# Graph layer with routed experts: sorted rows copied by SP run by run, shorter row rounds, carried tiles in one sequence

## Chip, cores and metric

One core of one Trainium2 chip. The metric is the device time of one execution in microseconds. Before the change it is 2572.58 us (median of 3 runs, 2572.57 to 2572.97).

## What is computed

One layer over 6250 nodes of 256 features and 206250 edges sorted by destination:

```python
xn = layernorm(x)
x = x + graph_attention(xn, src, dst) + linear_attention_mix(xn)
z = layernorm(x) * gamma + beta
logits = z @ Wr + br                       # 8 experts
top_vals, top_idx = top_k(logits, 2); w = softmax(top_vals)
y = sum over both picks of w * (gelu(z @ W1[e] + b1[e]) @ W2[e] + b2[e])
x = x + y
```

The graph attention has 4 heads of 64: each edge fetches its source row, gets a softmax weight among the edges of its destination, and is added to it. The last three lines are the routed experts (256 to 512 to 256).

## The kernel before

**Edge loop.** The edges are cut into 403 blocks of 512. For block n, POOL issues four indirect gathers (L1113, 128 rows of 264 floats each) into one of four buffers; it first waits until PE is through with block n - 4 (`block_ps`). DVE forms logits (L1542 to L1544), ACT takes the exponential (L1179), DVE adds the former block to the accumulator (L1558, twice), weighs the selection matrix (L1550) and prepares the mask three blocks ahead (L1530 to L1534), and PE multiplies, 32 small products (L1303). Each engine's program is in order, written out by hand. After the steps of a block (`body`) come whatever other steps have that block's number: up to block 151 those of the mixing stage, from block 152 (FREE_FROM) the row rounds and the carried tiles.

**Row rounds.** Destinations are finished in order, so finished nodes leave the loop in rounds of 7 tiles of 128 rows (SIZES; the seventh has 4, the eighth 3). A round has steps u = 0 to 35, one a block from its start in STARTS: u 0 SP issues 16 loads of sums and two of rows (`sums`, `sync`, L261 to L268); u 4 ACT scales (28 activations, L314); u 5 DVE adds and inverts (L388, L389); u 6 ACT scales again (28, L321); u 7 DVE adds (L393), SP stores; u 8, 9 statistics (L397); u 10, 11 the deviation; u 12 to 28 in pairs of tiles: ACT normalizes into `sent_rows` (L331), PE turns the tile, PE multiplies by Wr, DVE reads the logits (L410); u 29, 30 DVE picks two experts; u 31 PE counts; u 32, 33 DVE works out each row's slot; u 35 the list of expert tiles that are full (`tile_list`). Rounds 0 to 5 start at blocks 152, 191, 230, 270, 309 and 349; round 6 (4 tiles) starts at 382 and has its steps packed into 18 blocks. Round 7 runs in the tail.

**Sending.** Each tile's rows go to `expert_in`, in which each expert has its own range, in two indirect scatters by POOL (`scatter`, L287), one for each row's first and second expert, 128 rows of 258 floats (the row, its node number, its gate). The table SENDS puts them behind POOL's gathers: one tile a block in the first 7 blocks of the next round.

**Carried tiles.** 28 of the 56 expert tiles of 256 rows are computed inside the loop (`carried_part`), seven after each list, at STARTS[q + 2] + 10, one every 5 blocks: SP loads rows and weights (L600 to L605), PE turns and multiplies, DVE copies b1 and gates and scales (L667 to L670), ACT applies gelu, DVE adds b2 and multiplies by the gate (L678, L679), SP stores (L610). The other 28 are computed in the tail, in which PE works and POOL gathers the carried results and adds the others to the output (L2152, L2162).

## Time and profile before

| | |
|---|---|
| median of the runs | 2572.58 us |
| profiled execution | 2576.69 us, of which the span of the core's instructions is 2575.0 us |
| busy | PE 1533.0 us (60%), DVE 1492.4 (58%), ACT 680.0 (26%), POOL 1852.0 (72%) |
| granted TensorE clock, mean | 0.672 of full speed |
| DMA | 441.85 MB, mean 172 GB/s; queue of POOL 35.9% of 16 engines' span, queue of SP and ACT 23.1% |

Busy times leave out register, semaphore and DMA-issuing instructions of SP and ACT. An indirect DMA of POOL counts as busy while POOL makes its descriptors. "Idle before" is the time for which the engine stood before an instruction, with what ended it; "issue" means that the profile shows nothing it waited for.

### The profile page before, as it was taken

What the parts mean: (1) busy time and instruction counts of PE and PEld (TensorE: products, weight loads), DVE (VectorE), ACT (ScalarE), POOL (GpSimd) and SP (SyncE); (2) the same over time, 40 slices, a digit from 0 to 9 for tenths busy, and PEclk for the clock granted to TensorE, in tenths of its full rate; (3) what the DMA queues carried; (4) which work ended last, traced back from release to release, by engine and by line L of the source; (5) the groups of instructions that cost most, each with busy time, mean ns of one, the idle gap of its engine ahead of it and who ended that gap; (6) DMA issues with size and microseconds to landing.
All of it is one profiled execution on the core that took longest, in us unless ns stands there. A gap on an engine that the chain in (4) does not pass through costs nothing. (4 is left out here: it accounts for less than half of the span.)

```text
span 2575.0 us, 53300 instructions
## 1 busy us (share of the span) xinstructions
PE 1533.0 (60%) x17219; PEld 1189.0 (46%) x17219; DVE 1492.4 (58%) x5566; ACT 680.0 (26%) x2013; POOL 1852.0 (72%) x1872
## 2 busy tenths in 40 slices
PE   5676665556666445335425664765675475648993
PEld 4444434444444333224324553554564364537882
DVE  5666656667777565444645665575567666534333
ACT  3332221122222131032123224323322433322220
POOL 1677777777777777777777777777777777746673
PEclk9688865666555555555556775777676676778997
DMA  9477775645555644544456675557557656557986
GB/s 303 130 205 200 199 202 145 177 113 144 161 155 149 166 118 109 150 118 108 109 146 174 181 206 169 160 162 202 171 162 206 198 164 192 163 167 201 249 225 205
DMA packets 301706, 441.85 MB, mean 172 GB/s; under 512 B 73686, under 2 KB 227752, under 8 KB 301292
## 3 DMA queue, kind: packets, MB, share of 16 engines
q0 software_dynamic: 94320, 246.50, 35.9%
q1 hardware_dynamic: 197980, 183.38, 23.1%
q10 hardware_dynamic: 9120, 8.48, 1.0%
q8 instruction: 141, 2.31, 0.4%
q14 instruction: 145, 1.19, 0.1%
HBM read 361.39 MB, written 72.13 MB: 168 GB/s over the span
## 5 line engine op out<-in xcount | busy, mean ns | idle before, releaser
L1113 POOL DMA_INDIRECT region<-node_table,src_idx x1612 | 1576.0, 978 | 503.2 <-issue 475.1
L1303 PE MATMUL ps_p<-region 128*32 128x65 f32 x12896 | 389.3, 288 | 440.7 <-DVE region L1550 438.4
L1303 PEld LDWEIGHTS ps_p<-region 128*32 128x32 f32 x12896 | 301.0, 150 | 540.7 <-DVE region L1550 531.8
L1285 PE MATMUL ps_s<-ident,region 128*128 128x128 f32 x403 | 167.5, 416 | 427.3 <-DVE region L1544 417.2
L1179 ACT ACTIVATE ps_p<-region 128x16 f32<-128x16 f32 x403 | 75.4, 187 | 1249.6 <-DVE region L1544 1242.7
L1558 DVE SCALAR_TENSOR_TENSOR acc<-ps_p,region,acc 128x65 f32 x806 | 193.2, 280 | 285.2 <-issue 279.2
L1550 DVE TENSOR_TENSOR region<-region,ps_p 128x512 f32<-128x512 f32 x403 | 273.5, 679 | 49.9 <-ACT ps_p L1179 48.3
L1285 PEld LDWEIGHTS ps_s<-ident,region 128*128 128x128 f32 x403 | 87.7, 217 | 458.7 <-DVE region L1544 447.2
L1542 DVE TENSOR_TENSOR region<-region,ps_s 128x16 f32<-128x16 f32 x403 | 68.0, 169 | 284.5 <-DMA region<-node_table,src_idx 248.6
L1289 PEld LDWEIGHTS ps_s<-region 128*128 128x128 f32 x806 | 199.6, 278 | 60.9 <-issue 34.9
L1175 ACT ACTIVATE region<-ps_s 128x128 f32<-128x128 f32 x403 | 111.1, 276 | 303.7 <-PE ps_s L1285 303.3
L1289 PE MATMUL ps_s<-region 128*128 128x32 f32 x806 | 189.7, 325 | 0.2 <-ACT region L1175 0.2
L1531 DVE SCALAR_TENSOR_TENSOR region<-drep,region 128x8 f32<-128x8 f32 x403 | 91.7, 228 | 64.5 <-DVE region L1530 64.5
L2227 PE MATMUL ps_eu<-region 128*128 128x256 f32 x448 | 112.7, 409 | 24.1 <-DVE region L2271 17.3
L287 POOL DMA_INDIRECT expert_in<-acc x98 | 100.6, 1027 | 30.1 <-issue 30.1
L2162 POOL DMA_INDIRECT out_dram<-acc,rows_of x56 | 90.7, 1620 | 42.8 <-issue 42.5
L1530 DVE TENSOR_SCALAR region<-drep,region 128x8 f32 x403 | 103.2, 256 | 20.5 <-issue 15.6
L1534 DVE TENSOR_TENSOR region<-region 128x128 f32<-128x128 f32 x403 | 114.3, 284 | 0.0
L2227 PEld LDWEIGHTS ps_eu<-region 128*128 128x128 f32 x448 | 91.7, 207 | 41.2 <-DVE region L2271 18.8
L1319 PE MATMUL ps_x<-region 128*128 128x384 f32 x196 | 106.3, 680 | 0.0
L2239 PE MATMUL ps_ey<-region 128*128 128x256 f32 x448 | 101.3, 379 | 0.0
L2152 POOL DMA_INDIRECT acc<-y_rows,acc x70 | 70.0, 1000 | 41.7 <-issue 20.7
(347 smaller groups left out, 2477.5 us busy)
## 6 DMA issues: line engine op xcount, KB each, us to landing
region<-in_W_dram SPq DMA_DIRECT2D x84, 512.0 KB, 5.5
region<-node_table,src_idx POOLq DMA_INDIRECT x1612
acc<-in_W_dram SPq DMA_DIRECT2D x28, 512.0 KB
region<-expert_in SPq DMA_DIRECT2D x47, 258.0 KB, 5.6
acc<-base_rows SPq DMA_DIRECT2D x13, 896.0 KB, 7.3
qkv_rows<-region SPq DMA_DIRECT2D x49, 194.0 KB
y_rows<-acc SPq DMA_DIRECT2D x28, 256.0 KB
node_table<-region SPq DMA_DIRECT2D x49, 132.0 KB, 4.7
```

The source lines that it names most:

```text
L1113: pool.indirect_dma_start(out=rows[:, s, j, :], out_offset=None, in_=table[:, :], in_offset=bass.IndirectOffsetOnAxis(ap=src_idx[:, n * SU ...
L1175: act.activation(maskT[:, s % 2, :], ps_s[s % 2][:, 0:P], ACT.Copy).then_inc(maskT_ready, 1)
L1285: pe.transpose(ps_s[s % 2][:, 0:P], mask[:, s % SL].rearrange("p j w -> p (j w)"), ident[:, :]).then_inc(maskT_ps, 1)
L1289: pe.matmul(ps_s[s % 2][:, 2 * P:2 * P + SUB * 8], maskT[:, s % 2, :], dsel[:, s % SL].rearrange("p j c -> p (j c)"), start=True, stop=Tru ...
L1303: m = pe.matmul(ps_p[s % 2][h * WIN:(h + 1) * WIN, 0:HC], wts[:, s % 2, j, h, :], rows[:, s, j, h * HC:(h + 1) * HC], start=j == 0, stop=j ...
L1319: m = pe.matmul(ps_x[2 + a % 2][:, 0:3 * HID], xT_tiles[:, a % XT, c, :], w_q[:, c, :], start=c == 0, stop=c == KC - 1)
L1530: own.do(dve.tensor_scalar(t8[:, 0, :], drep[:, bass.ds(c, 1), :].squeeze(1), here[:, 0, at(n)], None, ALU.mult))
L1534: own.do(dve.tensor_tensor(mask[:, s % SL], bcast(rel[:, bass.ds(n * SUB, SUB)], 2, WIN), bcast(win, 1, SUB), ALU.is_equal))
L1550: dve.tensor_tensor(wts[:, s % 2], bcast(mask[:, s], 2, G_HEADS), bcast(ex_ps(s), 3, WIN), ALU.mult).then_inc(w_ready, 1)
L1558: m = dve.scalar_tensor_tensor(out=a, in0=ps_p[s % 2][:, 0:HC], scalar=here[:, k, at(n)], in1=a, op0=ALU.mult, op1=ALU.add)
L2227: m = pe.matmul(ps_u[2 * (n % 2) + f // 2][:, (f % 2) * MT:(f % 2 + 1) * MT], w1s[n % WS][:, c, f * P:(f + 1) * P], xeT[:, n % 2, c, :], s ...
L2239: m = pe.matmul(ps_y[n % 2][:, b * DIM:(b + 1) * DIM], hidT[:, n % 2, c, b * P:(b + 1) * P], w2s[n % WS][:, c, :], start=c == 0, stop=c == ...
```

## The change

Rounds 0 to 4 (35 tiles) no longer scatter through POOL. Behind u 33 of such a round each tile is sorted by expert: DVE builds a 128 x 256 selection matrix from the two picks (steps 33 + 2j), PE multiplies it with the tile in two halves (34 + 2j, 35 + 2j), ACT copies each half out of PSUM (35 + 2j, 36 + 2j), SP writes 256 sorted rows to `run_rows` in DRAM (37 + 2j). Then SP copies, expert by expert, 128 rows from where that expert's run begins to where its next free slot begins, DRAM to DRAM, with both addresses from a register: 8 copies a tile, two a block (`send_runs`). The rows beyond the run's end are overwritten by the next tile's, so a half of four experts waits until the same half of the tile before has landed. Rounds 5, 6 and 7 still scatter (now one row buffer for both picks).

A row now holds 260 floats: the values, node number, first expert, second weight, and first minus second weight. The carried part and the tail work out the gate from these (`weigh_rows`, two more DVE operations a tile, with an own column of `b1T` for the expert's number). The steps u 0 to 33 of rounds 0 to 4 are packed into 22 blocks (table AT), several in one block, and the rounds start at 152, 189, 226, 263 and 300; round 5 stays at 349 and round 6 at 382. The 28 carried tiles stand in one sequence, every 5 blocks from block 257 to 392. At the front, SP loads b1 in four pieces and fills the spare rows of `run_rows`, 0.9 MB.

```diff
-MROW = DIM + 2
+MROW = DIM + 4
+TURNED = 5
+TURN_U = 33
+SLOT = 5 * P
...
+        j = turn(r, u, 4)
+        if j is not None:
+            m = r.m + j
+            turned_out.wait(sp, 2 * (m + 1))
+            if m >= GT:
+                for half in run_out:
+                    half.wait(sp, HALF_RUNS * (m - GT + 1))
+            sp.dma_start(run_rows[j * SLOT:j * SLOT + 2 * P, :].rearrange("(c p) d -> p c d", p=P),
+                         sorted_rows[:, m % 2]).then_inc(run_in[m % 2].sem, 16)
     part.sync = sync
+
+    def send_runs(sp, r, q):
+        j, part_of = divmod(q, 4)
+        m = r.m + j
+        if part_of == 0:
+            run_in[m % 2].wait(sp, 16 * (m // 2 + 1))
+        landed = run_out[part_of // 2]
+        if m and part_of % 2 == 0:
+            landed.wait(sp, HALF_RUNS * m)
+        for e in range(2 * part_of, 2 * part_of + 2):
+            v = sp.value_load(run_at[0:1, j * E + e:j * E + e + 1], min_val=0, max_val=N_PAD * 512 + 511)
+            to = expert_in[e * CAP:(e + 1) * CAP, :][bass.ds(v >> 9, P), :]
+            sp.dma_start(to.rearrange("(a b) c -> a (b c)", a=16),
+                         run_rows[j * SLOT:(j + 1) * SLOT, :][bass.ds(v & 511, P), :].rearrange("(a b) c -> a (b c)", a=16)).then_inc(landed.sem, 16)
+    part.send_runs = send_runs
...
+    def turn(r, u, d):
+
+        k = u - TURN_U - d
+        return k // 2 if r.turned and 0 <= k < 2 * r.gt and k % 2 == 0 else None
+
+    def turn_half(r, u, d):
+
+        k = u - TURN_U - d
+        return divmod(k, 2) if r.turned and 0 <= k < 2 * r.gt else None
...
-            act.activation(sent_rows[:, j, :, 0:DIM], bcast(x_all[:, j, :], 1, 2), ACT.Identity,
+            act.activation(sent_rows[:, j, 0:DIM], x_all[:, j, :], ACT.Identity,
...
+        j = turn_half(r, u, 2)
+        if j is not None:
+            j, c = j
+            m = r.m + j
+            turned.wait(act, 2 * m + c + 1)
+            if m >= 2 and c == 0:
+                run_in[m % 2].wait(act, 16 * (m // 2))
+            act.activation(sorted_rows[:, m % 2, c, :], ps[3][:, 0:MROW], ACT.Copy).then_inc(turned_out.sem, 1)
...
+        j = turn_half(r, u, 1)
+        if j is not None:
+            j, c = j
+            m = r.m + j
+            if c == 0:
+                chosen.wait(pe, m + 1)
+            if m or c:
+                turned_out.wait(pe, 2 * m + c)
+            pe.matmul(ps[3][:, 0:MROW], sel[:, m % 2, c * P:(c + 1) * P], sent_rows[:, j, :], start=True, stop=True).then_inc(turned.sem, 1)
...
+            if r.turned:
+                if r.m:
+                    runs_landed(dve, r.m)
+                runs = run_te.rearrange("p (t e) -> p t e", e=E)[:, 0:n]
+                spot3 = spot_te.rearrange("p (t e) -> p t e", e=E)[:, 0:n]
+                own.do(dve.tensor_tensor_scan(run_te, mask_te[:, :], ps[3][:, DIM:DIM + n * E], 0.0, ALU.mult, ALU.add))
+                own.do(dve.tensor_tensor(runs, runs, total, ALU.subtract))
+                own.do(dve.tensor_tensor(spot3[0:1], pos[0:1], bcast(cap[0:1, :], 1, n), ALU.subtract))
+                own.do(dve.scalar_tensor_tensor(out=run_at[0:1, :], in0=spot_te[0:1, :], scalar=512.0, in1=run_te[0:1, :], op0=ALU.mult, op1=ALU.add))
+                own.do(dve.tensor_tensor(spot3, runs, ps[3][:, 0:n * E].rearrange("p (t e) -> p t e", e=E), ALU.add))
...
+                if r.turned:
+                    own.do(dve.tensor_tensor(work, oh, spot_te.rearrange("p (t e) -> p t e", e=E)[:, 0:n], ALU.mult))
+                    own.do(dve.tensor_reduce(spots[:, c, 0:n], work, AX.X, ALU.add))
...
+        j = turn(r, u, 0)
+        if j is not None:
+            m = r.m + j
+            if m >= 2:
+                turned.wait(dve, 2 * (m - 1))
+            own.do(dve.tensor_scalar(sel[:, m % 2, :], spot[:, :], spots[:, 0, j:j + 1], None, ALU.is_equal))
+            dve.scalar_tensor_tensor(out=sel[:, m % 2, :], in0=spot[:, :], scalar=spots[:, 1, j:j + 1], in1=sel[:, m % 2, :],
+                                     op0=ALU.is_equal, op1=ALU.add).then_inc(chosen.sem, 1)
...
+def weigh_rows(dve, own, gates, choice, expert):
+
+    own.wait()
+    own.do(dve.scalar_tensor_tensor(out=gates, in0=choice[:, :, 0], scalar=expert, in1=choice[:, :, 2], op0=ALU.is_equal, op1=ALU.mult))
+    own.step(dve.tensor_tensor(gates, gates, choice[:, :, 1], ALU.add))
...
-    CARRY_AT, CARRY_STEP = 10, 5
-    STARTS = [FREE_FROM + d for d in (0, 39, 78, 118, 157, 197)]
-    STEPS = {s + u: [(k, u)] for k, s in reversed(list(enumerate(STARTS))) for u in range(ROWS_U)}
+    CARRY_AT, CARRY_STEP = BLOCKS - 146, 5
+    STARTS = [FREE_FROM + d for d in (0, 37, 74, 111, 148, 197)]
+    AT = (0, None, None, None, 3, 3, 5, 5, 6, 6, 7, 8, 9, 9, 10, 10, 11, 11, 12, 12, 13, 13, 14, 14, 15, 15, 16, 16, 17, 17, 18, 19,
+          20, 21)
+    TURN_AT = AT[TURN_U]
+    STEPS, RUN_STEPS = {}, {}
+    for k, s in enumerate(STARTS):
+        if k < TURNED:
+            for u in range(TURN_U + 4 + 2 * GT):
+                d = AT[u] if u < len(AT) else TURN_AT + u - TURN_U
+                if d is not None:
+                    STEPS.setdefault(s + d, []).append((k, u))
+            for q in range(4 * GT):
+                RUN_STEPS[s + TURN_AT + 5 + q] = (k, q)
+        else:
+            for u in range(ROWS_U):
+                STEPS.setdefault(s + u, []).append((k, u))
...
-    for k in range(EARLY - 2):
-        for j in range(SIZES[k]):
-            SENDS.setdefault(STARTS[k + 1] + j, []).append((k, j))
...
-            for q in range(4):
-                d = n - v - STARTS[q + 2] - CARRY_AT
-                if 0 <= d < CARRY_STEP * CARRY and d % CARRY_STEP == 0:
-                    return q * CARRY + d // CARRY_STEP
-            return None
...
+                if n in RUN_STEPS:
+                    k, q = RUN_STEPS[n]
+                    part.send_runs(sp, early_round(k), q)
                 m = carry_at(n, -2)
                 if m is not None:
-                    carried.sync(sp, m, (m // CARRY + 2) * (2 * GT * 16))
+                    carried.sync(sp, m, (m // CARRY + 2) * GT)
```

POOL's order behind the front of the program, before: gathers for the edges (L1113) and scatters to expert_in (L287), here the last two tiles of one round and the first of the next.

```order
L287 DMA expert_in<-acc 54272x258 x2
L1113 DMA region<-node_table,src_idx 128x264 x4
L287 DMA expert_in<-acc 54272x258 x2
L1113 DMA region<-node_table,src_idx 128x264 x132
L287 DMA expert_in<-acc 54272x258 x2
```

And with the change, where L1244 is the gather and L332 the scatter:

```order
L1233 MEMSET acc 128x1792 x2
L1244 DMA region<-node_table,src_idx 128x264 x1552
L332 DMA expert_in<-acc 54272x260 x4
L1244 DMA region<-node_table,src_idx 128x264 x4
L332 DMA expert_in<-acc 54272x260 x4
```

The first 388 blocks' gathers now follow one another with nothing between.

ACT's order at the start of round 0, before: L1179 and L1175 are the exponential and the mask's copy of a block, L314 and L321 the 28 scalings of u 4 and u 6.

```order
L314 ACTIVATE acc<-acc,w_self 128x65 x28
L1179 ACTIVATE ps_p<-region 128x16
L1175 ACTIVATE region<-ps_s 128x128
L1179 ACTIVATE ps_p<-region 128x16
L1175 ACTIVATE region<-ps_s 128x128
L321 ACTIVATE acc<-acc 128x64 x28
L1179 ACTIVATE ps_p<-region 128x16
L1175 ACTIVATE region<-ps_s 128x128
```

And DVE's order there with the change: the end of the body of block 3 (L1665, L1666), u 5 (L464, L465), then the next body (L1674 on).

```order
L1665 TENSOR_TENSOR region<-bm,region 128x32
L1666 TENSOR_TENSOR region<-region 128x128
L464 TENSOR_TENSOR acc<-acc 128x1820
L465 RECIPROCAL acc<-acc 128x28
L1674 TENSOR_TENSOR region<-region,ps_s 128x16
L1675 SCALAR_TENSOR_TENSOR region<-region 128x16
```

Before, u 5 stood one body behind the block in which ACT does u 4; now it stands at the end of that same block, and u 7 likewise in the block of u 6.

## Rows read from the trace of the kernel before

**Rows 1.** Page, groups: line, engine, operation, count | busy us, mean ns | idle before, releaser

```profile
L1113 POOL DMA_INDIRECT region<-node_table,src_idx x1612 | 1576.0, 978 | 503.2 <-issue 475.1
```

**Rows 2.** Timeline of POOL: start us, us, instruction [idle before <- releaser]

```profile
726.05 0.95 POOL L1113 DMA_INDIRECT region<-node_table,src_idx  x1 [1.93 <-PE ps_p L1303]
...
1069.33 0.95 POOL L1113 DMA_INDIRECT region<-node_table,src_idx  x1 [0.30 <-issue]
1070.58 1.01 POOL L287 DMA_INDIRECT expert_in<-acc  x1 [0.31 <-issue]
```

**Rows 3.** Waits (us in total, times, longest): whole run; 873:1452; 1452:2271

```profile
POOL region L1113 <- PE ps_p L1303: 20.2, 52, 1.9
...
DVE region L1542 <- DMA region<-node_table,src_idx: 141.2, 68, 7.0
...
DVE region L1542 <- DMA region<-node_table,src_idx: 50.1, 27, 5.3
```

**Rows 4.** POOL's groups in 873:1452 and 1452:2271; windows (PE, PEld, DVE, ACT, POOL busy, PEclk, DMA, GB/s)

```profile
L1113 POOL DMA_INDIRECT region<-node_table,src_idx x424 | 414.0, 977 | 129.2 <-issue 123.1 <-PE ps_p L1303 6.1
L287 POOL DMA_INDIRECT expert_in<-acc x28 | 27.9, 996 | 8.5 <-issue 8.5
...
L1113 POOL DMA_INDIRECT region<-node_table,src_idx x575 | 561.3, 976 | 175.2 <-issue 171.9 <-PE ps_p L1303 3.4
L287 POOL DMA_INDIRECT expert_in<-acc x56 | 57.9, 1034 | 17.1 <-issue 17.1
...
873.00:1452.00 579.00, 262.57 (x3903) 200.56 (x3904) 302.76 (x1222) 138.80 (x470) 441.30 (x452) 0.53 0.49 137
1452.00:2271.00 819.00, 504.38 (x6128) 407.19 (x6126) 509.78 (x1968) 262.36 (x731) 619.25 (x631) 0.70 0.61 177
2271.00:2575.00 304.00, 224.64 (x1094) 192.75 (x1094) 112.22 (x312) 64.29 (x153) 176.19 (x142) 0.87 0.77 217
```

**Rows 5.** Timeline: logits and products of one block; logits of another and the next

```profile
895.81 0.17 DVE L1542 TENSOR_TENSOR region<-region,ps_s 128x16 f32<-128x16 f32 x1 [3.25 <-DMA region<-node_table,src_idx]
...
898.19 1.09 PE L1303 MATMUL ps_p<-region 128*32 128x65 f32 x32 [1.26 <-DVE region L1550]
...
1179.15 0.17 DVE L1542 TENSOR_TENSOR region<-region,ps_s 128x16 f32<-128x16 f32 x1 [1.41 <-DMA region<-node_table,src_idx]
...
1184.17 0.17 DVE L1542 TENSOR_TENSOR region<-region,ps_s 128x16 f32<-128x16 f32 x1 [1.72 <-DMA region<-node_table,src_idx]
```

**Rows 6.** DVE's groups in 1452:2271: steps of the rounds and the carried tiles

```profile
L670 DVE TENSOR_SCALAR acc<-ps_x,affine 128x256 f32<-128x256 f32 x49 | 24.3, 537 | 0.2 <-issue 0.2
...
L678 DVE TENSOR_TENSOR acc<-ps_x,acc 128x512 f32<-128x512 f32 x26 | 18.0, 692 | 6.3 <-PE ps_x L654 2.5 <-DVE region L1534 2.1 <-DVE acc L444 0.9
L397 DVE BATCH_NORM_STATS2 acc<-acc 128x6 f32<-128x256 f32 x25 | 8.6, 412 | 0.6
...
L667 DVE COPY acc<-b1T 128x4 f32 x24 | 4.9, 203 | 23.0 <-DVE region L1534 11.3 <-issue 4.1 <-DVE acc L410 2.9
...
L437 DVE TENSOR_TENSOR acc<-acc 128x56 f32<-128x56 f32 (+1 forms) x10 | 2.1, 214 | 0.9
```

**Rows 7.** Timeline at u 4 and u 5 of round 0

```profile
897.14 6.81 ACT L314 ACTIVATE acc<-acc,w_self 128x65 f32<-128x65 f32 x28
...
904.04 0.69 DVE L1550 TENSOR_TENSOR region<-region,ps_p 128x512 f32<-128x512 f32 x1 [2.83 <-ACT ps_p L1179]
...
905.99 2.06 DVE L388 TENSOR_TENSOR acc<-acc 128x1820 f32<-128x1820 f32 x1
906.32 2.55 POOL L1113 DMA_INDIRECT region<-node_table,src_idx  x1 [0.30 <-issue]
```

**Rows 8.** Timeline at the start of round 6, of 4 tiles

```profile
2150.43 0.17 DVE L1542 TENSOR_TENSOR region<-region,ps_s 128x16 f32<-128x16 f32 x1
2152.17 10.33 SPq L261 DMA_DIRECT2D acc<-acc  x16
...
2170.38 3.95 ACT L314 ACTIVATE acc<-acc,w_self 128x65 f32<-128x65 f32 x16 [6.84 <-DMA acc<-base_rows]
```

More of the change, by code:

```diff
@@ L204 @@
 EARLY_TILES = sum(SIZES[:EARLY])
-MAIN_SENT = sum(SIZES[:EARLY - 1])
+MAIN_TURNED = sum(SIZES[:TURNED])
+MAIN_SENT = sum(SIZES[TURNED:EARLY - 1])
+HALF_RUNS = 8 * EXPERTS
 EARLY_PAIRS = pairs_in(SIZES[:EARLY])
@@ L275, in sync @@
         elif u == 8:
-            if r.k:
+            if r.m:
+                turned.wait(sp, 2 * r.m)
+            if r.s:
                 sp.wait_ge(sent, 32 * r.s)
@@ L281, in sync, with runs_landed @@
             sp.wait_ge(n_ready, r.t + n)
-    part.sync = sync
+        j = turn(r, u, 4)
[7 more added lines that the diff above has]
+                         sorted_rows[:, m % 2]).then_inc(run_in[m % 2].sem, 16)
+    part.sync = sync
+    def send_runs(sp, r, q):
[12 more added lines that the diff above has]
+    part.send_runs = send_runs
+    def runs_landed(eng, tiles):
+        for half in run_out:
+            half.wait(eng, HALF_RUNS * tiles)
     def scatter(pool, r, j):
@@ L353, in tensor @@
             pe.wait_ge(n_ready, r.t + (j + 1))
+            if j == 0 and r.m:
+                turned_out.wait(pe, 2 * r.m)
             if j >= 2:
@@ L415, in vector @@
             pick(dve, own, n, lg, 0, first)
+            own.do(dve.tensor_copy(sent_rows[:, 0:n, DIM + 1], gate))
         elif u == 30:
@@ L552, in list_at @@
     if q < 4:
[L553 removed]
+        return g["carry_e"][:, q, :], g["carry_s"][:, q, :]
     first = sum(LISTS[4:q])
@@ L590, in carried_part, with sync @@
     carried.first_landed = first_landed
-    def sync(sp, m, sent_count):
+    def sync(sp, m, tiles):
         q, s = m // CARRY, m % 2
         listed.wait(sp, q + 1)
-        sp.wait_ge(sent, sent_count)
-        v = sp.value_load(carry_s[0:1, q % 2, m % CARRY:m % CARRY + 1], min_val=0, max_val=EXPERTS * CAP + (EXPERTS - 1) * MT)
+        for half in run_out:
+            half.wait(sp, HALF_RUNS * tiles)
+        v = sp.value_load(carry_s[0:1, q, m % CARRY:m % CARRY + 1], min_val=0, max_val=EXPERTS * CAP + (EXPERTS - 1) * MT)
         if m >= 2:
@@ L672, in vector @@
             i.then_inc(xeT_ready.sem, 1)
+            weigh_rows(dve, own, gates[:, m % 4, :], choice[:, m % 4], b1s[:, m % 4, FC:])
         elif v == 8:
@@ L915, in main_stage @@
         row_loads = sem("row_loads")
+        g["row_sems"].update(chosen=Since(stats, X_GROUPS), turned=Since(sqrts, X_GROUPS), turned_out=Since(weights, 2),
+                             run_in=[Since(table_out[i], 16 * XG * ((X_GROUPS + 1 - i) // 2)) for i in range(2)],
+                             run_out=[Since(src_in, 16), Since(dst_in, 32)])
         part = rows_part(g, g["row_sems"], ps_x)
@@ L1392, in _ @@
                     carry_sems["listed"].wait(pe, LISTED)
+                    part.turned_out.wait(pe, 2 * MAIN_TURNED)
                     send_notes(g, pe, ps_x[3], noted_ps)
@@ L1844, in round_of @@
                     part.sums(sp, early_round(k, 1))
-                    for u in range(ROWS_U):
+                    for u in range(TURN_U + 4 + 2 * GT):
                         part.sync(sp, early_round(k, 1), u)
+                        j, due = divmod(u - TURN_U - 5, 2)
+                        if k < TURNED and 0 <= j < GT and due == 0:
+                            for q in range(4 * j, 4 * j + 4):
+                                part.send_runs(sp, early_round(k, 1), q)
                 for k in range(EARLY - 1):
@@ L1870, in rest @@
             def rest():
-                for k in range(EARLY - 1):
+                for k in range(TURNED, EARLY - 1):
                     for j in range(SIZES[k]):
@@ L1890, in round_of @@
                 def round_of(k):
-                    for u in range(ROWS_U):
+                    for u in range(TURN_U + 4 + 2 * GT):
                         part.scalar(act, early_round(k, 1), u)
@@ L1917, in round_of @@
                 def round_of(k):
-                    for u in range(ROWS_U):
+                    for u in range(TURN_U + 4 + 2 * GT):
                         part.tensor(pe, early_round(k, 1), u)
@@ L1973, in round_of @@
                 def round_of(k):
-                    for u in range(ROWS_U):
+                    for u in range(TURN_U + 4 + 2 * GT):
                         part.vector(dve, own, early_round(k, 1), u)
@@ L2273, in rows_back @@
                 m.then_inc(xeT_ready, 1)
+                weigh_rows(dve, own, gates[:, n % MS, :], choice[:, n % MS], b1s[:, n % MS, FC:])
             def result(n):
```

121 lines of the change are left out of this document (74 added, 47 removed).

## The prediction

> **What bounds the kernel now.** I read the page's groups of instructions, then the waits of the whole run and of two stretches, then single blocks in the timeline. The edge loop runs 403 blocks, and POOL issues four gathers for each. The idle time ahead of its gathers is "issue" for 475 of 503 us [rows 1]: it waits for nobody, it needs 0.95 us for a gather and 0.30 us to reach the next [rows 2]. PE holds it up for 20.2 us in all [rows 3]. So in the loop a thing taken off POOL's queue is worth its issue time, as long as DVE keeps pace. That condition decides here, so I split the free part of the loop where the carried tiles become dense.
>
> Stretch A (873 to 1452 us, blocks 152 to 256, 105 blocks): 579 us, of which DVE waits 141.2 us for gathered rows [rows 3]. DVE's chain (its own work, and what it waits for from ACT and PE) needs 579 - 141 = 438 us. Stretch B (1452 to 2271 us, blocks 257 to 402): 819 us, DVE waits for gathers only 50.1 us [rows 3], so the chain needs 769. POOL's own need without any scatter, and without its waits for PE, is 579 - 36.4 - 6.1 = 537 us in A and 819 - 75.0 - 3.4 = 741 in B: the window less busy and idle time of L287 and less PE's part of L1113's [rows 4]. **In A POOL has 99 us over DVE; in B, without scatters, DVE's chain is the longer one already, 769 against 741.**
>
> **What goes.** 70 scatters leave POOL: all 28 of A's and 42 of B's 56; the order shows the last 14 alone between gathers. One costs 36.4/28 = 1.30 us in A and 75.0/56 = 1.34 in B [rows 4]: 36.4 and 56.2 us, 92.6 together. In B at most the 50 us of gather waits can come away, even if nothing were added.
>
> **What is added on DVE's chain.** A block without other steps takes it 1184.17 - 1.72 - 1179.15 = 3.3 us [rows 5]; of the 5.03 us that POOL gives a block, 1.7 are free in A.
> - Selection: two operations over 128x256 a tile. I take 0.8 us for both with their waits, nearest to two of L397 at 0.41; bounds 0.5 and 1.4 (two at 0.69) [rows 6]. Further small steps in u 29, 32 and 33, about ten at 0.21 [rows 6] plus gaps: 2.7. A turned round: 7 x 0.8 + 2.7 = 8.3 us.
> - weigh_rows: two small operations and a wait, 0.5 us a carried tile, 14 for 28.
> - Three more carried tiles fall into B (28 against 25). One is two of L670 at 0.54, two of L678 at 0.69 and two small ones at 0.2, 2.9 us of work [rows 6]; with its waits (23.0/24 = 1.0 ahead of L667 alone) I take 5: 15 us.
> - **Compression puts u4 with u5, and u6 with u7, in one block.** ACT's 28 scalings take 6.8 us and begin 897.14 - 895.81 = 1.3 us behind DVE's logits [rows 5, 7]. Before, DVE did a block meanwhile and lost only the late exponential, 2.8 us ahead of L1550 [rows 7]. Now it stands until 8.1 us instead of 3.3: 4.8 us each time, net 2 more.
> - u4 comes 3 blocks after the loads, not 4. At the one place where it came after 2, SP issued from 2152.17 and ACT could start at 2170.38: 18.2 us [rows 8]. SP starts 1.8 us after the block's logits (2150.43), so data are there 20 us behind them; three blocks are 15.1, and with ACT's 1.3 the new wait is 3.6 us in A, about 3 in B.
>
> B's chain: 769 + 2 rounds x 8.3 + 1.6 (last turns of round 2) + 14 + 15 + 2 x (2 x 2 + 3) = 830, less 13 for the end of round 2 (u 29 to 35, some 50 small steps at 0.21 and a gap), which moves ahead of block 257, plus 10 for the gather waits that stay where DVE is not late: 827. **B: +8 us.**
>
> A: POOL's 537, plus stalls. POOL may be four blocks ahead: from the end of a block's gathers to the first that needs its buffer are 0.3 + 3 x 5.03 = 15.4 us, and PE's products end 898.19 + 1.09 - 895.81 = 3.5 us after a block's logits begin [rows 5], so DVE may be 11.9 us late. It is 1.8 us late when all is well. Blocks 3 to 6 of a compressed round take 4.9 + 6.8 + 2.4 = 14.1, 3.3, 1.3 + 6.8 + 2.4 = 10.5, and 3.3 + 7 x 0.41 + 6 x 0.21 = 7.5 us [rows 5 to 7] (L393 and L321 taken like L388 and L314): 35.4 against 20.1, so 15.3 later, 17.1 in all, 5.2 over the limit. Such a stall exists now, 1.93 us [rows 2]. Three rounds: 16 us. With 2 us for a late chain at the boundary: 555. **A: -24 us.**
>
> Outside the loop: the tail's 28 tiles are paced by PE (busy 225 of 304 us [rows 4]); weigh_rows hides there, unless DVE becomes late, 0.5 us a tile, 14 at most. I take 0. The loads at the front hide behind the mixing stage: 0 to 5.
>
> **Work off the chain.** SP issues 280 copies. A plain issue is 10.33/16 = 0.65 us [rows 8]; even at twice that for the register loads, two a block are 2.6 of 5 us, so SP holds. A copy moves 128 x 260 x 4 = 133 KB; 35 tiles x 8 are 37 MB read and 37 written, with run_rows' own 266 KB 1.33 MB a tile read. That is about 45 GB/s more on A's 137 and 28 on B's 177, at DMA shares of 0.49 and 0.61 [rows 4]: no bound; a gather may land later, which four buffers cover in A. PE gets two 128x260 products a tile, an estimated 0.5 us each, with PE busy 263 of 579 us in A and 504 of 819 in B [rows 4].
>
> A gather that meets DVE's 2.06 us sum over 128x1820 takes 2.55 instead of 0.95 us [rows 7]. The Trainium skill (SBUF — State Buffer, "SBUF: two separate sides") says why: DVE and GpSimd share one port pair, held for a whole instruction. The trace agrees. By it all 70 new selections would hit POOL, up to 0.8 us a tile, 28 us, 17 of them in A. The rows bound it lower: L1113 averages 978 ns against 950 over all that DVE does [rows 1, 2], 0.03 us a gather, so under 2 us here, left out.
>
> Moving the scatters to SP saves issue time alone, and issue time is what POOL is short of: 1.3 us each [rows 4]. The Trainium skill (DMA: Bandwidth & Descriptors, "Issuing engines are not separate DMA queues") speaks against the change: another issuing engine saves only the sequencer's time, "usually small relative to the DMA itself". The rows do not agree for POOL; by the rule alone the sum would be about 0.
>
> **Sum.** -24 + 8 = -16 us, on the profiled execution's 2576.69 us: 2560.7. The median of the runs is 4.1 us below that execution, so I predict **2556.5 us**. A measurement of this kernel can tell 0.2%, 5 us.
>
> **Rivals.**
> - *Inputs late (slower).* Each round's 18 loads share SP and the rings with the former round's copies, and my row (18.2 us) is of a 4-tile round; 7-tile loads with copies ahead could be 5 to 9 us longer. DVE stands behind ACT in that block, so 5 rounds x 5 to 9 us = 25 to 45: 2582 to 2602. It decides from 16/5 = 3 us a round. For: SP's waits sit in one queue. Against: in round 0, of 7 tiles, ACT found the data after four blocks without a wait [rows 7]. Chance 0.25.
> - *Added work hides (faster).* ACT's and PE's part in B's 769 is waiting, and what is inserted falls into it: B's chain grows by 15, not 58, so B gives -30, all -54 with A: 2518 to 2535. Chance 0.17.
> - *POOL alone counts.* All 92.6 come away, 2480. Against it stand B's 50 us. Chance 0.03.
> - *No change.* Gains and costs cancel within 5 us, by contention, the port or the tail. Chance 0.13.
> - My forecast, 2540 to 2567: 0.42.
>
> The range that leaves out 2 in 10 is 2525 to 2590. Faster by over 0.2%: 0.42 + 0.17 + 0.03 = 0.62; same 0.13; slower 0.25.
>
> **What would show it.** In the profile after, the gathers' group keeps 0.98 us and its "issue" time, but waits for PE 40 to 100 us, against 20 now, in bursts 5 to 10 blocks after each round's start; 28 scatters instead of 98; DVE's wait for gathers falls from 141 to about 60 in A and from 50 to about 10 in B; block 257 comes near 1428 us, 24 earlier, the loop's end near 2255, only 16 earlier. If POOL waits for PE under 20 us in all, the chain was priced too high and the time is near 2500; if ACT's first scaling waits over 8 us for its loads in each round, the slower rival holds.

## The result and the profile after

The changed kernel takes **2589.49 us** (median of 4 runs), the kernel before 2572.57 on the same chip: a ratio of 1.0058, 95% interval 1.0043 to 1.0073. It is slower by 17 us where I forecast 16 faster. The profiled execution has a span of 2587.5 us.

The gathers' group on the page after, beside [rows 1], with the queue that takes SP's copies (packets, MB, share of 16 engines) and the group of DVE's first operation on gathered rows:

```profile
q1 hardware_dynamic: 217420, 231.05, 28.9%
...
L1244 POOL DMA_INDIRECT region<-node_table,src_idx x1612 | 1576.0, 978 | 615.2 <-issue 471.1
...
L1674 DVE TENSOR_TENSOR region<-region,ps_s 128x16 f32<-128x16 f32 x403 | 68.0, 169 | 164.5 <-DMA region<-node_table,src_idx 120.0
```

A gather costs what it did, 978 ns, and POOL's "issue" (idle for which the profile shows no cause) is 471.1 us against 475.1. What grew is the rest of the idle time: 615.2 - 471.1 = 144 us, against 28 before. POOL is rid of 70 scatters and now waits for others.

The waits of stretch A (872 to 1438 us, blocks 152 to 256) and of B (1438 to 2288, blocks 257 to 402), beside [rows 3] (who <- whom: us, times, longest):

```profile
DVE region L1674 <- DMA region<-node_table,src_idx: 59.0, 38, 4.6
DVE acc L464 <- ACT acc L371: 34.4, 3, 12.6
POOL region L1244 <- PE ps_p L1434: 28.8, 10, 3.5
ACT acc L371 <- DMA acc<-base_rows: 19.9, 3, 7.6
```

```profile
POOL region L1244 <- PE ps_p L1434: 99.2, 38, 9.5
DVE acc L464 <- ACT acc L371: 36.4, 3, 18.5
PEld ps_x L742 <- DMA region<-expert_in: 22.3, 2, 13.6
ACT acc L371 <- DMA acc<-base_rows: 14.3, 2, 8.4
DVE region L1674 <- DMA region<-node_table,src_idx: 8.6, 3, 4.6
```

DVE's waits for gathers fell to 59.0 and 8.6, as forecast (60 and 10). But L371, ACT's scalings of u4, now waits for the row loads in rounds 0 to 3 (7.6, 6.9, 5.4 and 8.4 us; the fifth wait, 5.9, is round 6's, which had one before too). L742, PE's transposes of a carried tile's rows, waits 13.6 us in one place. POOL's groups in the two stretches, beside [rows 4]:

```profile
L1244 POOL DMA_INDIRECT region<-node_table,src_idx x424 | 411.5, 971 | 155.2 <-issue 126.4 <-PE ps_p L1434 28.8
```

```profile
L1244 POOL DMA_INDIRECT region<-node_table,src_idx x576 | 562.9, 977 | 263.5 <-issue 164.3 <-PE ps_p L1434 99.2
L332 POOL DMA_INDIRECT expert_in<-acc x14 | 13.8, 982 | 4.3 <-issue 4.3
```

Block by block (from the timeline, the start of DVE's first operation on a block's logits) the time went like this. The rows begin at the starts of rounds 0, 1, 2, 4 and 5 and at block 257, where B begins; round 3 starts at 263. The last three columns are experiments, of which more below; their control is the column "again", c1_after.

| blocks | before | change | again | c3_lead2 | c2_all | e5_scatters |
|---|---|---|---|---|---|---|
| 152 to 189 | 189.3 | 198.4 | 197.4 | 191.5 | 190.0 | 197.6 |
| 189 to 226 | 208.3 | 197.6 | 197.9 | 194.1 | 189.8 | 208.2 |
| 226 to 257 | 182.1 | 169.6 | 170.2 | 164.5 | 166.0 | 177.2 |
| 257 to 300 | 235.9 | 248.1 | 246.7 | 261.7 | 246.1 | 246.9 |
| 300 to 349 | 274.9 | 300.9 | 304.4 | 291.4 | 283.4 | 295.9 |
| 349 to 402 | 308.0 | 300.5 | 302.1 | 300.1 | 304.5 | 306.5 |
| sum | 1398.4 | 1415.2 | 1418.8 | 1403.3 | 1379.8 | 1432.4 |

A is 14 us faster (forecast 24), B is 31 us slower (forecast 8). 26 of B's 31 lie in blocks 300 to 349; of the rest, 12 were lost in 257 to 300 and 7.5 won back behind 349.

A round's start in the timeline: round 0, block 152, whose logits are at 872.32; block 155's are at 888.2 (start, us, engine, line, idle before):

```profile
874.13 11.54 SPq L276 DMA_DIRECT2D acc<-acc  x16
885.71 0.60 SPq L282 DMA_DIRECT2D acc<-node_table  x1
886.36 0.66 SPq L283 DMA_DIRECT2D acc<-base_rows  x1
...
897.25 6.82 ACT L371 ACTIVATE acc<-acc,w_self 128x65 f32<-128x65 f32 x28 [7.62 <-DMA acc<-base_rows]
...
904.10 2.06 DVE L464 TENSOR_TENSOR acc<-acc 128x1820 f32<-128x1820 f32 x1 [12.57 <-ACT acc L371]
904.73 2.25 POOL L1244 DMA_INDIRECT region<-node_table,src_idx  x1 [0.30 <-issue]
```

From SP's first issue to ACT's start are 23.1 us, with no copies of an earlier round about; I had taken 18.2 from a 4-tile round. The second run of the same kernel (c1_after) has 21.7 there. ACT starts u4 9.1, 8.4, 6.8, 10.0 and 15.0 us behind the block's logits in rounds 0 to 4, and 9.7 in the uncompressed round of block 349; with data in time it is 1.3. In rounds 0 to 3 the row loads release it, in the last two PE does. The block with u4 and u5 takes 18.6, 17.9, 16.3, 19.5 and 26.6 us, forecast 14.1.

Round 4, block 300, whose logits are at 1686.03, is the dearest. A carried tile's rows (L709) are asked for in the same block as the row loads:

```profile
1687.79 12.08 SPq L276 DMA_DIRECT2D acc<-acc  x16
1699.91 0.60 SPq L282 DMA_DIRECT2D acc<-node_table  x1
1700.55 0.66 SPq L283 DMA_DIRECT2D acc<-base_rows  x1
1702.33 2.25 SPq L321 DMA_DIRECT2D expert_in<-run_rows  x2
1705.50 0.41 SPq L709 DMA_DIRECT2D region<-expert_in  x1
...
1709.28 5.78 SPq L321 DMA_DIRECT2D expert_in<-run_rows  x4
1712.22 0.71 PEld L742 LDWEIGHTS ps_x<-ident,region 128*128 128x128 f32 x4 [13.62 <-DMA region<-expert_in]
...
1713.91 0.28 ACT L1306 ACTIVATE region<-ps_s 128x128 f32<-128x128 f32 x1 [14.02 <-PE ps_s L1416]
1714.08 6.80 ACT L371 ACTIVATE acc<-acc,w_self 128x65 f32<-128x65 f32 x28
```

The request leaves SP's queue 19.5 us after the block's logits, behind 18 loads and two copies. PE stands until it lands; ACT stands behind PE's transposes, DVE behind ACT. A sequence of step 5 meets them at 300 and, one block off, at 350 (8.7 us at 2014). Before, the carried tiles were tied to the rounds' starts, and one request alone fell behind row loads of its own block: at 382, the same 4-tile round from which I read the loads' time. There PE waited 6.2 us:

```profile
2164.59 0.39 SPq L600 DMA_DIRECT2D region<-expert_in  x1
...
2171.15 0.71 PEld L633 LDWEIGHTS ps_x<-ident,region 128*128 128x128 f32 x4 [6.19 <-DMA region<-expert_in]
```

### The profile page after: what moved, and what is told of

It reads as the page before. It is cut to its first block and busy times, and to the rows that moved or that the text cites. A ratio compares the mean times of both kernels' runs of the same rounds, so it can differ in the third digit from the quotient of the medians.

```text
span 2587.5 us, 56527 instructions
## 1 busy us (share of the span) xinstructions
PE 1584.4 (61%) x17359; PEld 1232.6 (48%) x17359; DVE 1546.6 (60%) x5813; ACT 690.4 (27%) x2083; POOL 1780.0 (69%) x1803
## 5 line engine op out<-in xcount | busy, mean ns | idle before, releaser
L1244 POOL DMA_INDIRECT region<-node_table,src_idx x1612 | 1576.0, 978 | 615.2 <-issue 471.1
L1416 PEld LDWEIGHTS ps_s<-ident,region 128*128 128x128 f32 x403 | 95.4, 237 | 428.4 <-DVE region L1676 419.7
L1420 PEld LDWEIGHTS ps_s<-region 128*128 128x128 f32 x806 | 205.9, 280 | 59.1 <-issue 27.9
L1420 PE MATMUL ps_s<-region 128*128 128x32 f32 x806 | 182.2, 316 | 0.0
L1674 DVE TENSOR_TENSOR region<-region,ps_s 128x16 f32<-128x16 f32 x403 | 68.0, 169 | 164.5 <-DMA region<-node_table,src_idx 120.0
L1666 DVE TENSOR_TENSOR region<-region 128x128 f32<-128x128 f32 x403 | 114.5, 284 | 0.0
L2380 PEld LDWEIGHTS ps_ey<-region 128*128 128x128 f32 x448 | 83.9, 192 | 10.8
```

Source lines behind the costliest of these rows:

```text
L1244: pool.indirect_dma_start(out=rows[:, s, j, :], out_offset=None, in_=table[:, :], in_offset=bass.IndirectOffsetOnAxis(ap=src_idx[:, n * SU ...
L1416: pe.transpose(ps_s[s % 2][:, 0:P], mask[:, s % SL].rearrange("p j w -> p (j w)"), ident[:, :]).then_inc(maskT_ps, 1)
L1420: pe.matmul(ps_s[s % 2][:, 2 * P:2 * P + SUB * 8], maskT[:, s % 2, :], dsel[:, s % SL].rearrange("p j c -> p (j c)"), start=True, stop=Tru ...
L1666: own.do(dve.tensor_tensor(mask[:, s % SL], bcast(rel[:, bass.ds(n * SUB, SUB)], 2, WIN), bcast(win, 1, SUB), ALU.is_equal))
L2380: m = pe.matmul(ps_y[n % 2][:, b * DIM:(b + 1) * DIM], hidT[:, n % 2, c, b * P:(b + 1) * P], w2s[n % WS][:, c, :], start=c == 0, stop=c == ...
```

## The experiments

The experiments ran on five chips, of two kinds. On one the kernel before takes 2577 us, near the 2573 of the prediction; c1, c2, c3 and e5 ran there. On four others, the slower chips, it takes 2969 to 3010, 15 to 17% more in every run. Ratios are to the kernel before on the same chip.

| run | edit | before, us | this, us | ratio (95%) |
|---|---|---|---|---|
| c1_after | the change again | 2577.4 | 2596.5 | 1.0075 (1.0050 to 1.0099) |
| c3_lead2 | u4 on two blocks later | 2577.4 | 2583.5 | 1.0022 (1.0008 to 1.0037) |
| c2_all | all three edits | 2577.4 | **2555.2** | 0.9916 (0.9894 to 0.9939) |
| e5_scatters | scatters kept | 2577.4 | 2608.2 | 1.0122 (1.0100 to 1.0145) |
| k1_after | the change again | 3000.9 | 2979.1 | 0.9929 (0.9912 to 0.9945) |
| e1_lead2 | u4 on two blocks later | 3009.5 | 2979.2 | 0.9896 (0.9875 to 0.9918) |
| e2_carry3 | carried tiles 3 blocks earlier | 3009.5 | 2986.7 | 0.9921 (0.9904 to 0.9937) |
| c4_carry3 | same | 3003.6 | 2978.7 | 0.9919 (0.9898 to 0.9941) |
| e3_split | double steps apart | 3009.5 | 2953.1 | 0.9809 (0.9793 to 0.9825) |
| c5_split | same | 3003.6 | 2948.5 | 0.9816 (0.9799 to 0.9832) |
| k2_split | same | 3000.9 | 2950.8 | 0.9830 (0.9814 to 0.9847) |
| m1_split | same | 2969.1 | 2912.8 | 0.9803 (0.9774 to 0.9832) |
| e4_all | all three | 3009.5 | 2947.4 | 0.9790 (0.9774 to 0.9807) |
| e6, k3, m2 | all three, scatters kept | 3003.6, 3000.9, 2969.1 | 3002.4, 3002.3, 2973.2 | 0.9996, 1.0003, 1.0012 |
| e7_early, k4_early | loads and carried rows earlier | 3003.6, 3000.9 | 2939.1, 2940.3 | 0.9785, 0.9796 |

**Loads further ahead.** The steps from u4 on come two blocks later, the loads stay:

```diff
-    AT = (0, None, None, None, 3, 3, 5, 5, 6, 6, 7, 8, 9, 9, ...
+    AT = (0, None, None, None, 5, 5, 7, 7, 8, 8, 9, 10, 11, 11, ...
```

> The changed kernel, whose steps from u 4 on come two blocks later in the five compressed rounds (u 4 and 5 at block 5 after the row loads, not 3); u 0, the loads, stay. Theory 'inputs late': the 18 loads land 24 us behind the block's logits, so ACT waits 7.6, 6.9, 5.4 and 8.4 us for them in rounds 0 to 3. Then these waits fall under 1 us, PE's products are held up less and POOL's waits for PE in blocks 152 to 256 fall from 28.8 to 5 to 15 us; round 4 keeps the 13.6 us of PE's wait for the carried tile's rows. Time 2562 to 2577. Rival 'DVE's chain is too long anyway' (selection, weighing, carried tiles): the wait was cover for nothing and only moves, ACT's waits go but the time stays within 5 us of 2589. Rival 'loads are slowed by the copies': they still land after 5 blocks, ACT still waits over 3 us.

> As e1_lead2 (u 4 and later steps two blocks later), on this chip: late inputs give 12 to 27 us less than the changed kernel beside it, and ACT's waits of 7.6, 6.9, 5.4 and 8.4 us for the loads in rounds 0 to 3 fall under 1; if these waits only covered DVE's own length, within 5 us of it.

It took 13 us off its control (2596.5 to 2583.5). Stretch A and its waits in c1_after, then in c3_lead2:

```profile
L1244 POOL DMA_INDIRECT region<-node_table,src_idx x423 | 412.2, 975 | 153.5 <-issue 126.0 <-PE ps_p L1434 27.5
```

```profile
L1243 POOL DMA_INDIRECT region<-node_table,src_idx x423 | 413.0, 976 | 138.3 <-issue 126.8 <-PE ps_p L1433 11.5
```

ACT starts 1.3 us behind the logits in rounds 0 to 2, the double block is 10.8 us in all three (16.5, 17.6 and 18.5 in the control), POOL waits 16.0 us less for PE, and A is 15.5 us shorter (565.6 to 550.1). That settles A: late loads were its cause. B gained nothing, 853.2 us in both. The steps now met carried rows in round 3, where PE waited 6.5 us at 1484 for the first time, and 11.3 in round 4; blocks 257 to 300 got 15 us longer, 300 to 349 13 shorter. On a slower chip the edit gave 0.9896 (e1_lead2), against 0.9929 for the unedited change on another of them (k1_after).

**Carried tiles three blocks earlier**, `BLOCKS - 149` for `BLOCKS - 146`:

> The changed kernel with its sequence of 28 carried tiles three blocks earlier (first at block 254, not 257). Theory 'one sequence collides with the row loads': at block 300 the carried tile's rows are asked for in the same block as the row loads and stand behind their 18 issues in SP's queue, so PE waits 13.6 us for them, and again about 8 us at block 350. Then PE's wait for these rows falls from 22.3 us to under 4 and the time by 8 to 17 us: 2572 to 2581. Rival 'ACT would have waited for the row loads in that block anyway': PE's wait goes, ACT's first scaling of round 4 waits 8 us instead, the gain is 2 to 7 us, 2582 to 2588. Rival 'rings full': the rows land as late as before, no gain.

> As e2_carry3 (carried tiles from block 254, nothing else), where the kernel before takes 2573 to 2577. The changed kernel gives 1.0058 to 1.0075 of it. If PE's wait for the rows of the carried tile (22.3 us, of which 13.6 at block 302) is what row loads at 300 and 349 cost, 8 to 17 us less: a ratio of 0.999 to 1.003. c3_lead2 showed 4 other blocks of that kind appear when the rounds' steps move (PE waited 25.7 us there and stretch B gained nothing), so the other outcome, under 4 us less, is likelier than I thought: it would say that the rows are late wherever SP's queue has 18 loads ahead of them.

It ran only on the slower chips. In c4_carry3 PE's wait for the rows fell to 5.4 us (19.3 in k1_after), and the time did not move against that control (0.9919 and 0.9921, 0.9929). There the wait goes and nothing is gained that these comparisons, each on its own chip, could show. The third outcome (the rows land as late as before) is out, since the wait went. ACT's wait for the row loads rose from 8.8 to 14.1, which speaks for the second. On the faster chip it was not tried alone.

**Double steps apart**: u4, 5, 6, 7 in blocks 3, 4, 5, 6, all later ones a block later.

```diff
-    AT = (0, None, None, None, 3, 3, 5, 5, 6, 6, 7, 8, ...
+    AT = (0, None, None, None, 3, 4, 5, 6, 7, 7, 8, 9, ...
```

> The changed kernel with u 4 and 5, and u 6 and 7, in separate blocks (3, 4, 5, 6 after the loads), all later steps one block later. By the term of my sum (4.8 us each time DVE stands behind ACT's 28 scalings, net 2 more than apart) DVE gets the body of a block meanwhile: 5 rounds x 2 x 2 = 20 us off DVE's chain, of which POOL shows what is over its slack: 8 to 20 us, 2570 to 2582. Theory 'inputs late' alone: ACT's wait for the loads stays 5 to 10 us a round since u 4 stays where it is, and gives 2578 to 2586. Rival 'no effect, the block behind needs ACT's exponential in any case': within 5 us of 2589.

> As e3_split (u 4, 5, 6, 7 in blocks of their own, the loads three blocks ahead as in the changed kernel). c2_all took 41 us off the changed kernel and c3_lead2 13, so splitting and the earlier carried tiles share 28 us. If DVE's standing behind ACT's 28 scalings was the larger part, this gives 15 to 28 us less than the changed kernel (ratio to the kernel before 0.996 to 1.001), with ACT's waits for the loads unchanged at 5 to 9 us but DVE's wait for ACT before u 5 (34.4 us in A, 36.4 in B) under 10 in each. If lateness is all, under 8 us.

> u 4, 5, 6, 7 in blocks of their own, nothing else. On the two slower chips it gave most of what all three edits gave (0.981 and 0.9816 against 0.979). Where the kernel before takes 2573 to 2577: if the double steps are the larger part, 15 to 28 us less than the changed kernel, 0.996 to 1.001; if late loads are, under 8 us less, over 1.003.

> u 4, 5, 6, 7 in blocks of their own, nothing else; k1_after and k2_split showed 28 us for it where the kernel before takes 3001 (2979 to 2951). Where it takes 2573 to 2577: with the double steps as the larger part 15 to 28 us less than the changed kernel, 0.996 to 1.001, and PE's wait for carried rows in stretch B still about 20 us; with late loads as the larger part over 1.003. On a slower chip again: 0.983.

It ran only on the slower chips, four times. On one of them the control ran too, 2979.1 to 2950.8: 28 us. Waits of the whole run in k1_after, then in k2_split:

```profile
DVE acc L464 <- ACT acc L371: 38.0, 5, 13.1
POOL region L1244 <- PE ps_p L1434: 112.4, 45, 9.5
```

```profile
POOL region L1243 <- PE ps_p L1433: 85.1, 45, 4.9
```

DVE's waits for ACT before u5 are gone from the list, those before u7 fell from 24.6 to 3.1. ACT can still be late, but DVE has a block's products meanwhile. I had priced this at 2 us a time net, 20 in all; on the slower chips it is the largest of the three (0.9803 to 0.9830, against 0.9896 and 0.992 for the others). Over the five blocks from u4 on it gave 3.4, 3.0, 3.1 and 2.6 us in rounds 0 to 3, and 9.6 in round 4, where the late carried rows fall.

**All three together**, u4 to 7 in blocks 5, 6, 7, 8, later ones three blocks later, carried tiles from block 254:

> All three together: u 4, 5, 6, 7 in blocks 5, 6, 7, 8 after the loads, later steps three blocks later, carried tiles from block 254. If lateness of the loads, the collision and the double steps are what turned the forecast's -16 into +17, the parts add: -20, -12 and -12, 2540 to 2555, with POOL's waits for PE under 50 us (128 now in blocks 152 to 402) . If DVE's chain with selection and carried tiles is the cause, it stays over 2575.

> As e4_all (u 4 to 7 in blocks 5, 6, 7, 8 after the loads, carried tiles from block 254), on this chip: against the changed kernel beside it 35 to 45 us less if late inputs, the collision and the double steps are the cause, 2540 to 2555 where the kernel before takes 2573; under 15 us less if DVE's chain with selection and weighing is.

41 us less than the control, **and 0.9916 of the kernel before: it beats both**, as it does on the slower chip (0.979). POOL in stretch A and in B of c2_all:

```profile
L1243 POOL DMA_INDIRECT region<-node_table,src_idx x426 | 417.6, 980 | 129.8 <-issue 129.5 <-PE ps_p L1433 0.3
```

```profile
L1243 POOL DMA_INDIRECT region<-node_table,src_idx x574 | 565.9, 986 | 244.0 <-issue 159.0 <-PE ps_p L1433 85.0
```

In A POOL waits for nobody: 545.8 us for 105 blocks, the bound that I had put at 537, 9 us too low. In B it still waits 85.0 us; 834 us against 819 before. How the double block came apart in round 0, where ACT's exponential (L1309) of the next block is done before DVE needs u5:

```profile
904.41 0.19 ACT L1309 ACTIVATE ps_p<-region 128x16 f32<-128x16 f32 x1 [2.71 <-DVE region L1675]
904.94 0.28 ACT L1305 ACTIVATE region<-ps_s 128x128 f32<-128x128 f32 x1 [0.35 <-PE ps_s L1415]
905.12 6.80 ACT L371 ACTIVATE acc<-acc,w_self 128x65 f32<-128x65 f32 x28
911.82 0.17 ACT L1309 ACTIVATE ps_p<-region 128x16 f32<-128x16 f32 x1
```

From the logits of the block with u4, five blocks take 33.1 to 33.2 us in rounds 0 to 2 (36.4 to 37.1 in c3_lead2, 41.8 to 43.9 in the control). So with loads in time, taking two double blocks apart is worth 3.2 to 4.0 us a round here, 1.6 to 2.0 a time.

**The change without the moved scatters**: compression, one sequence, weighing kept, rows sent by POOL as before.

```diff
-TURNED = 5
+TURNED = 0
...
-            for q in range(4 * GT):
-                RUN_STEPS[s + TURN_AT + 5 + q] = (k, q)
...
+    for k in range(EARLY - 2):
+        for j in range(SIZES[k]):
+            SENDS.setdefault(STARTS[k + 1] + j, []).append((k, j))
```

> The changed kernel with its rounds compressed, its one sequence of carried tiles and the weighing kept, but rows sent by POOL's scatters as before (one tile a block from the next round's start) and no sorting, no copies by SP. It separates what compression and sequence cost from what turning and the copies bring. POOL gets 70 scatters of 1.3 us back, 92 us; DVE loses five turned rounds at my 8.3, 42 us, PE and SP their part. If the copies do what they are for, this is slower than the changed kernel, by the 92 us less what POOL waits for PE there (28.8 + 99.2 us in blocks 152 to 402): 2600 to 2640. If turning costs DVE as much as the scatters cost POOL, within 8 us of 2589. If turning and the copies are what made the change slower, under 2580.

2608.2 against 2596.5: the moved scatters are worth 12 us here, and without them the schedule and the weighing cost 31 us over the kernel before. POOL in its stretch A, then in B:

```profile
L1244 POOL DMA_INDIRECT region<-node_table,src_idx x421 | 410.7, 976 | 137.2 <-issue 123.4 <-PE ps_p L1434 13.8
L332 POOL DMA_INDIRECT expert_in<-acc x28 | 28.0, 1000 | 8.5 <-issue 8.5
```

```profile
L1244 POOL DMA_INDIRECT region<-node_table,src_idx x579 | 566.0, 978 | 199.4 <-issue 169.4 <-PE ps_p L1434 30.0
L332 POOL DMA_INDIRECT expert_in<-acc x56 | 60.2, 1076 | 17.1 <-issue 17.1
```

Its B takes 849.3 us, 30.6 over the kernel before, and POOL waits 30.0 us for PE there, against 3.4 in [rows 4]: POOL bounded B before, and the new schedule's waits lengthened it. With the scatters moved (c1_after) POOL waits 27.5 + 102.0 us, not 13.8 + 30.0: 86 us of the 96 taken off its queue (113.8 for 84 scatters here, 18.1 for the 14 left there) came back as waiting for PE. A is 17.5 us shorter, B 3.9 longer.

The run shows one thing more. In its rounds 1 to 3 the row loads are in time, and ACT starts 1.2 to 1.3 us behind the logits: the first blocks of these rounds hold scatters, and three of them take 24.2 to 24.9 us. In the changed kernel three take 14.1 to 16.2. **The scatters were also the time in which the loads landed**, so the 12 us are their worth less the lateness that moving them caused.

> c2_all (all three edits) but with POOL's scatters in place of sorting, products and SP's copies, as in e5_scatters. It tells what moving the scatters is worth when nothing holds POOL up. By the forecast's terms: in stretch A POOL waits for PE only 0.3 us in c2_all, so all 28 scatters come back at 1.3, +36 us; in B DVE's chain is 4 x 8.3 shorter and POOL has 42 scatters more, 56 us: -5 to +15. Together 2586 to 2606, 31 to 51 over c2_all. If the copies in the rings cost gathers and loads more than was seen, the difference is under 20.

> All three edits, but scatters by POOL, no sorting, no copies. Where the kernel before takes 2573 to 2577: 31 to 51 us over c2_all's 0.9916, so 1.003 to 1.012. If the turning with its copies gives nothing once the loads are early, it is within 8 us of c2_all.

> All three edits with POOL's scatters, no sorting, no copies. Where the kernel before takes 2573 to 2577: 31 to 51 us over c2_all's 0.9916, so 1.003 to 1.012, if the scatters come back as issue time of POOL; within 8 us of c2_all if turning costs as much as it gives. On a slower chip again: 1.000, 61 us over the all-edits version.

With all three edits the scatters cost 0.9996 to 1.0012 against 0.979 (e4_all, on another of the slower chips), about 60 us of 3000. On the faster one this was not measured.

**A version meant to be better still**: as c2_all, but row loads two blocks earlier in place of later steps, and a carried tile's rows asked for four blocks ahead; round 5's steps u 4 to 28 also come one block later, and the carried tiles start at block 256.

```diff
-    STARTS = [FREE_FROM + d for d in (0, 37, 74, 111, 148, 197)]
+    STARTS = [FREE_FROM + d for d in (0, 35, 72, 109, 146, 197)]
...
+                m = carry_at(n, -4)
+                if m is not None:
+                    carried.sync_rows(sp, m, (m // CARRY + 2) * GT)
                 m = carry_at(n, -2)
                 if m is not None:
-                    carried.sync(sp, m, (m // CARRY + 2) * GT)
+                    carried.sync(sp, m)
```

> A version meant to beat both. As c2_all, but the row loads of rounds 1 to 4 come two blocks earlier instead of their later steps two later (starts 35, 72, 109, 146 blocks after the first), round 5's u 4 to 28 one block later, carried tiles from block 256, and SP asks for a carried tile's rows four blocks ahead instead of two (its weights still two). In c2_all the loads still landed 28 to 32 us behind the block's logits in stretch B and PE waited 17.3 us for carried rows. If SP's order of issue is what makes both late, PE's wait falls under 6, ACT's waits in rounds 3 to 5 under 4 each, and the time by 8 to 20 us: 2535 to 2548. If DVE's own chain is the bound of stretch B by now, within 5 us of c2_all's 2555.

> The version meant to beat both, on this chip. Where the kernel before takes 2573 to 2577: 2535 to 2550, 0.985 to 0.990, with PE's wait for carried rows under 6 us (17.3 in c2_all). If DVE's own chain bounds stretch B by now, 0.990 to 0.993.

PE's waits for carried rows are gone from its list, and the time is that of e4_all (0.9785 and 0.9796, 0.979): on these chips nothing more was won with them. On the faster chip it was not run.

**The controls.**

> The changed kernel as it is, run again as the control of the edits beside it: the chip of the first four runs gave 3010 us for the kernel before, 17% over its 2573, so edits of the changed kernel are to be compared with the changed kernel on the same chip. On a chip as the first: 1.006 of the kernel before.

> The changed kernel again as control. Where the kernel before takes 2573 to 2577 us: 1.006 of it. Where it takes 3004 to 3010 us (two of the three chips of the experiments; there every wait for PE ends about 1 us after PE's record, and a free block takes 6.2 us, not 5.03) POOL is held to DVE's pace anyway, and taking scatters off it is worth little: the edits gave 0.979 to 0.992 of the kernel before there, so for the unedited change I expect 0.996 to 1.006.

k1_after gave 0.9929, below the 0.996 that I expected at best: **on the one slower chip where it ran unedited the change is faster by 0.7%**; in the two comparisons in which the kernel before takes 2573 and 2577 us it is slower by 0.6 and 0.7%.

## Why the prediction was wrong

It said -24 in A and +8 in B, 2556.5 in all; measured are -14 and +31. Chance 0.62 stood on faster. The result lies in the span of the rival *Inputs late* (2582 to 2602) and half a us inside the stated range. That rival's own sign, ACT's first scaling over 8 us late for its loads in each round, came in round 3 alone (8.4): it was right for A, and had part of B.

- **The step that failed** is "data are there 20 us behind" the block's logits, and with it "the new wait is 3.6 us in A, about 3 in B". In rounds 0 to 3, where the row loads released it, ACT began 24.9, 24.1, 23.0 and 24.1 us behind the logits of the round's first block. Behind u4's normal 1.3 us the waits are 7.8, 7.1 and 5.5 in A, and 8.7 in round 3. Over the forecast that is 9.6 us in A, where the sum missed by 10. POOL's stalls, 16 us in the sum, were 28.8, and 537 + 28.8 is A's measured 566. In A c3_lead2 showed it to be the cause. The row it came from was of a 4-tile round; 7 tiles take 21.3 to 23.1 us from SP's first issue. The 7-tile case stood in the trace only as an upper bound, 24.5 us after the logits (ACT at 897.14 [rows 7], the logits at 872.66), and I read it as "without a wait". I had written the right bounds (5 to 9 us more, deciding from 3 a round) and given them a quarter. I had also overlooked that in rounds 1 to 5 the four blocks before u4 took 25.6 to 30.8 us, since scatters lay in them, and that the change takes these out.
- **Not in the sum at all**: a carried tile's request behind the row loads in SP's queue. I had counted the 28 tiles as work for DVE (15 us), not where SP issues them. It cost PE 13.6 and 8.7 us in B, and there ACT starts u4 13.7 and 8.4 us later than its 1.3, behind PE; the second is the round of block 349, which I had not charged at all. Together with round 3 ACT's late starts exceed the forecast by 24.8 us, near the 23 by which B missed, but that is arithmetic, not proof: c3_lead2 took 12 us off them and B did not get shorter. What is shown of B is that the three edits together take 19 us off it (853.2 to 834.0); their shares stay open.
- **The double block was sized about right.** Without the wait the sum has 10.5 us for u4/u5 (14.1 less 3.6) and 10.5 for u6/u7; with loads in time (c3_lead2, rounds 0 to 2) they are 10.8 and 10.4 to 10.7, from logits to logits. The net 2 us a time is 1.6 to 2.0 on the faster chip (c3_lead2 to c2_all). The 28 us of k2_split are more than the 20 of the sum in part through round 4 (9.6 of the 21.7 that the five blocks give in five rounds together). A reading of it, argued and not shown: apart, DVE works on while ACT stands behind PE or its loads. How c2_all's 41 us divide on the faster chip stays open beyond c3_lead2's 13.
- **Right**: the scatters are gone from POOL; the gathers' group kept its 0.98 us; DVE's gather waits are 59 and 8.6 (60 and 10). POOL's own need in A, 537, is 545.8 with nothing in its way (c2_all). Selection is 0.89 us (0.8), weighing 0.37 of work (0.5), a product 0.55 (0.5). The rows of B:

```profile
L440 PE MATMUL ps_x<-acc 128*128 128x260 f32 x66 | 30.1, 546 | 2.4 <-ACT acc L406 1.8
...
L543 DVE SCALAR_TENSOR_TENSOR acc<-spot,acc 128x256 f32<-128x256 f32 x16 | 8.0, 497 | 0.6
L542 DVE TENSOR_SCALAR acc<-spot,acc 128x256 f32<-128x256 f32 x16 | 6.2, 390 | 2.4
L661 DVE SCALAR_TENSOR_TENSOR acc<-acc 128x2 f32<-128x2 f32 x28 | 5.9, 211 | 0.0
L662 DVE TENSOR_TENSOR acc<-acc 128x2 f32<-128x2 f32 x28 | 4.6, 163 | 1.0
```

- **B's form** ("DVE's chain is the longer one already") held in this: POOL's waits for PE rose from 3.4 to 99.2 us there. "Waits for PE 40 to 100 us" in the whole run was too low; they are 136.2.
- **SP.** A copy takes 2.25/2 = 1.1 to 5.78/4 = 1.4 us of SP's queue, about the 1.3 that I took as twice a plain issue. Two a block did not bound a free block: in c2_all's A POOL waits 0.3 us for PE. But two of them stood ahead of the late carried request.
- **The rule of the Trainium skill** (DMA: Bandwidth & Descriptors, "Issuing engines are not separate DMA queues"), that another issuing engine saves only the sequencer's time: by it the sum would have been about 0. The runs do not agree for POOL's indirect DMAs. Measured are 12 us for the moved scatters in the schedule as changed and, with all three edits, about 60 of 3000 on the slower chips.
- **The port.** The gather at DVE's sum takes 2.25 us (2.55 before), and the gathers' mean did not rise. Of the 35 gathers that meet a selection's second operation (L543), 8 take 1.15 to 1.16 us and most of the others 0.95: about 2 us in all, as the rows had bounded it.

## What to carry to other kernels

Ask of a compressed schedule first whether its inputs still land in time, and price them by a transfer of the same size: a bound "it was not late after four blocks" says nothing about three. When a stream of requests is moved to a fixed step, list on which of the issuing queue's long bursts each of them falls; one request behind 18 loads stopped three engines. Ask also what the removed work was cover for: the scatters lengthened the blocks in which the loads landed. Work taken off the engine with the shortest slack comes back as waiting unless the next chain has room: 96 us less gave 86 us more waiting, and with all three edits POOL's waits for PE in A and B fell from 129.5 to 85.3.
